# Attention scores that carry over in PSUM by differences of keys, with the maximum subtracted in the first two of eight key steps

## The reference

```
q = (x @ Wq.T).reshape(b, t, 8, 64)
kv_latent = x @ Wkv_down.T                       # 64 numbers for each token
k = (kv_latent @ Wk_up.T).reshape(b, t, 8, 64)
v = (kv_latent @ Wv_up.T).reshape(b, t, 8, 64)
scores = einsum('bqhd,bkhd->bhqk', q, k) * 64 ** -0.5
out = einsum('bhqk,bkhd->bqhd', softmax(scores, axis=-1), v)
return out.reshape(b, t, 512) @ Wo.T
```

## Time and profile before

| what | value |
|---|---|
| median of 3 runs | 1230.92 us (1229.14 to 1231.17) |
| profiled execution | 1230.1 us |
| its span (first to last instruction) | 1228.3 us |
| PE busy | 1016.4 us (83%), 5480 matmuls |
| DVE busy | 792.7 us (65%) |
| POOL busy | 676.9 us (55%) |
| ACT busy | 488.4 us (40%) |
| attention's blocks | from 237.7 us to about 1034 us of the span |

### The profile page before, as it was taken

The page is one execution under the profiler, slowest core; times in us unless marked ns, Lnnn a source line. Parts: engine busy times, 40 slices in busy tenths (PEclk is TensorE's granted clock), DMA queues, the critical chain, the costliest instruction groups (busy, mean ns, idle before and its releaser), DMA issues.

```text
span 1228.3 us, 17831 instructions
## 1 busy us (share of the span) xinstructions
PE 1016.4 (83%) x5480; PEld 586.1 (48%) x5481; DVE 792.7 (65%) x1211; ACT 488.4 (40%) x760; POOL 676.9 (55%) x385
## 2 busy tenths in 40 slices
PE   5839975499999989999998999998999999559800
PEld 4828842244444554444454444445455555538600
DVE  6565457657878746787873777877667744565431
ACT  1354431244444344444434444442445554344300
POOL 0025344277777627677644777773687785035371
PEclk9999956599999989999998999999999999669955
DMA  8055522000000100000010000001001000145453
GB/s 287 7 168 156 148 71 88 24 2 1 1 1 1 44 2 1 1 1 1 1 44 2 1 1 1 1 1 43 1 1 76 30 1 1 34 154 161 133 151 121
DMA packets 39484, 60.26 MB, mean 49 GB/s; under 512 B 5872, under 2 KB 33008, under 8 KB 38384
## 3 DMA queue, kind: packets, MB, share of 16 engines
q1 hardware_dynamic: 19424, 25.30, 5.8%
q0 software_dynamic: 6912, 18.88, 5.8%
q10 hardware_dynamic: 13072, 15.09, 3.5%
HBM read 30.81 MB, written 23.07 MB: 44 GB/s over the span
## 4 chain that ended last, share of the span: by engine, by line
PE 60%; DVE 11%; issue 9%; ACT 8%; POOL 7%; DMA 3%; ACTq 0%; DVEq 0%; POOLq 0%; SPq 0%
PE ps_o L928 14%; PE ps L913 9%; PE ps L560 6%; PE ps L720 5%; ACT arena_b L1120 5%; POOL arena_b L1322 5%; PE ps_x L700 4%; DVE maxes L726 3%; PE ps L916 3%; PE ps L1061 3%; PE ps L197 2%; PE ps_x L949 2%; ACT rows_store L476 2%; POOL arena_b L675 2%; PE ps L544 1%
## 5 line engine op out<-in xcount | busy, mean ns | idle before, releaser
L1322 POOL TENSOR_TENSOR arena_b<-arena_b 128x1024 f32<-128x1024 f32 x224 | 537.1, 2398 | 275.4 <-PE ps_o L928 168.7
L726 DVE TENSOR_REDUCE maxes<-ps 128x2 f32<-128x1024 f32 x256 | 311.7, 1218 | 184.0 <-PE ps L720 181.0
L1120 ACT ACTIVATE arena_b<-ps 128x1024 f32<-128x1024 f32 x256 | 255.8, 1024 | 190.7 <-PE ps L916 178.3
L928 PE MATMUL ps_o<-arena_b,latent_now 128*64 128x512 f32 x1024 | 261.6, 618 | 14.2 <-ACT arena_b L1120 5.3
L913 PE MATMUL ps<-q_split,keys_now 64*128 64x512 f32 x1536 | 223.5, 396 | 0.0
L509 POOL DMA_INDIRECT arena_b<-scaled_x,token_of x80 | 75.8, 947 | 178.5 <-issue 83.1
L913 PEld LDWEIGHTS ps<-q_split,keys_now 64*128 64x128 f32 x1536 | 147.1, 188 | 30.3 <-issue 2.4
L928 PEld LDWEIGHTS ps_o<-arena_b,latent_now 128*64 128x64 f32 x1024 | 53.1, 135 | 150.2 <-ACT arena_b L1120 132.9
L1239 DVE RECIPROCAL rows_store<-rows_store 128x256 f32<-128x256 f32 (+1 forms) x72 | 112.6, 1565 | 12.0 <-ACT rows_store L1131 12.0
L916 PE MATMUL ps<-q_shift 64*128 64x512 f32 x512 | 101.9, 393 | 0.0
L675 POOL DMA_INDIRECT arena_b<-sorted_y,slots x64 | 60.8, 950 | 67.2 <-DVE x_res L683 27.9
(11 more groups left out here) (175 smaller groups left out, 1127.1 us busy)
## 6 DMA issues: line engine op xcount, KB each, us to landing
sorted_y<-arena_b ACTq DMA_DIRECT2D x80, 128.0 KB
scaled_x<-rows_store SPq DMA_DIRECT2D x32, 256.0 KB, 2.1
x_res<-x_in SPq DMA_DIRECT2D x4, 1024.0 KB, 13.0
keys_now<-keys_next SPq DMA_DIRECT2D x4, 1024.0 KB, 4.6
out<-x_res SPq DMA_DIRECT2D x32, 128.0 KB
arena_a<-w_gu SPq DMA_DIRECT2D x1, 2048.0 KB, 16.0
arena_a<-w_gu ACTq DMA_DIRECT2D x1, 2048.0 KB, 7.7
arena_b<-scaled_x,token_of POOLq DMA_INDIRECT x80
```

Source lines behind the costliest of these rows:

```text
L726: nc.vector.tensor_reduce(maxes[:, 2 * m:2 * m + 2], ps[2][:, :, :], AX_X, ALU.max) \
L928: last = nc.tensor.matmul(ps_o[h, :], latent_now[:, kt, :], src, start=(kt == 0), stop=(kt == KT - 1))
L1120: nc.scalar.activation(dst, ps_s[n % 2][:, :, :], ACT.Exp, scale=SCALE).then_inc(sem("exp_done"), 1)
L1322: nc.gpsimd.tensor_tensor(t, t, probs[kt % PROBS].rearrange("p a n -> p (a n)"), ALU.add) \
```

## The change

The latents of key tile kt become differences: for kt = 0, 1 the key itself, from kt = 2 on the key minus the key 256 tokens (two tiles) before. As the two PSUM tiles are used in turn, tile kt is written on top of the scores of kt - 2 and not cleared; so the sum is again the score of kt, and the maximum subtracted in steps 0 and 1 stays in. The shift's pair (L916) is issued in steps kt = 0, 1 only, ahead of the other three. The maxima still need whole keys, which get tiles of their own. The differences are made by DVE from `row_pairs`, now in block 1, and take five instructions for half 0 and three for half 1.

```
+STRIDE = 2
+FIRST = STRIDE * P
+        q_shift = sb("q_shift", [P, SEQ + P], F32R)
+        keys_max_next = sb("keys_max_next", [P, SEQ], F32R)
+        keys_max_now = sb("keys_max_now", [P, SEQ], F32R)
+        key_diff = sb("key_diff", [P, HALF])
...
         def act_latents(act, nb, j, bank):
-            nc.scalar.activation(keys_next[:, 0, j * HALF:(j + 1) * HALF], bank, ACT.Copy).then_inc(sem("lat_hi"), 1)
+            nc.scalar.activation(keys_max_next[:, j * HALF:(j + 1) * HALF], bank, ACT.Copy).then_inc(sem("lat_hi"), 1)
-        def dve_keys_lo(dve, nb, j, bank):
-            nc.vector.tensor_tensor(keys_next[:, 1, cols], bank, keys_next[:, 0, cols].bitcast(F32), ALU.subtract) \
-                .then_inc(sem("lat_lo"), 1)
+        def dve_keys(dve, nb, j):
+            latent = row_pairs[:, :, :].rearrange("p j n -> p (j n)")
+            a = max(j * HALF, FIRST)
+            cols, back = slice(a, (j + 1) * HALF), slice(a - FIRST, (j + 1) * HALF - FIRST)
+            diff = key_diff[:, 0:(j + 1) * HALF - a]
+            dve.wait_ge(sem("lat_hi"), 2 * nb + j + 1)
+            if j == 0:
+                nc.vector.tensor_copy(keys_next[:, 0, 0:FIRST], keys_max_next[:, 0:FIRST].bitcast(F32)) \
+                    .then_inc(sem("key_hi"), 1)
+                nc.vector.tensor_tensor(keys_next[:, 1, 0:FIRST], latent[:, 0:FIRST],
+                                        keys_max_next[:, 0:FIRST].bitcast(F32), ALU.subtract) \
+                    .then_inc(sem("key_lo"), 1)
+            nc.vector.tensor_tensor(diff, latent[:, cols], latent[:, back], ALU.subtract).then_inc(sem("key_diff"), 1)
+            dve.wait_ge(sem("key_diff"), 2 * nb + j + 1)
+            nc.vector.tensor_copy(keys_next[:, 0, cols], diff).then_inc(sem("key_hi"), 1)
+            dve.wait_ge(sem("key_hi"), 3 * nb + j + 2)
+            nc.vector.tensor_tensor(keys_next[:, 1, cols], diff, keys_next[:, 0, cols].bitcast(F32), ALU.subtract) \
+                .then_inc(sem("key_lo"), 1)
         def pe_turn_latents(pe, nb, j, bank):
-            pe.wait_ge(sem("lat_f"), 2 * nb + j + 1)
-            pe.wait_ge(sem("lat_lo"), 2 * nb + j + 1)
+            pe.wait_ge(sem("lat_hi"), 2 * nb + j + 1)
...
-                    for key, query in ((k_hi, q_hi), (k_hi, q_lo), (k_lo, q_hi)):
+                    first = kt < STRIDE
+                    if first:
                         for a, h in enumerate(head_rows):
-                            nc.tensor.matmul(ps_s[n % 2][:, a, :], keys_now[h, key, k], query[h, p, q],
-                                             start=(key == k_hi and query is q_hi), stop=False)
-                    for a, h in enumerate(head_rows):
-                        last = nc.tensor.matmul(ps_s[n % 2][:, a, :], shift_ones[h, :], shift_row[h, q],
-                                                start=False, stop=True)
+                            nc.tensor.matmul(ps_s[n % 2][:, a, :], shift_ones[h, :], shift_row[h, q],
+                                             start=True, stop=False, skip_group_check=True)
+                    for key, query in ((k_hi, q_lo), (k_lo, q_hi), (k_hi, q_hi)):
+                        for a, h in enumerate(head_rows):
+                            last = nc.tensor.matmul(ps_s[n % 2][:, a, :], keys_now[h, key, k], query[h, p, q],
+                                                    start=False, stop=(kt >= KT - STRIDE and query is q_hi and key == k_hi),
+                                                    skip_group_check=True)
...
-                                pe_max(pe, (p + 1) % PAIRS, m, keys_next if p == PAIRS - 1 else keys_now,
+                                    if p == PAIRS - 1:
+                                        pe.wait_ge(sem("key_lo"), 3 * (b + 2))
+                                pe_max(pe, (p + 1) % PAIRS, m, keys_max_next if p == PAIRS - 1 else keys_max_now,
...
                         pieces(1)
-                        if not last_batch and p in (1, 2) and d == 0:
-                            dve_keys_lo(dve, b + 1, p - 1, ps_x[:, :])
+                        if not last_batch and p in (1, 2) and d == 1:
+                            dve_keys(dve, b + 1, p - 1)
...
-                for src, dst in ((keys_next, keys_now), (latent_next, latent_now)):
-                    sp.dma_start(dst[:, :, :].bitcast(F32), src[:, :, :].bitcast(F32)).then_inc(sem("batch_ready"), 16)
+                for src, dst in ((keys_next[:, :, :], keys_now[:, :, :]), (latent_next[:, :, :], latent_now[:, :, :]),
+                                 (keys_max_next[:, :], keys_max_now[:, :])):
+                    sp.dma_start(dst.bitcast(F32), src.bitcast(F32)).then_inc(sem("batch_ready"), 16)
+            sp.wait_ge(sem("key_lo"), 3)
```

More of the change, by code:

```diff
@@ L95, in build @@
         q_split = sb("q_split", [P, PAIRS, 2, SEQ], F32R)
-        q_shift = sb("q_shift", [P, 2, 2, SEQ], F32R)
+        q_shift = sb("q_shift", [P, SEQ + P], F32R)
+        keys_max_next = sb("keys_max_next", [P, SEQ], F32R)
+        keys_max_now = sb("keys_max_now", [P, SEQ], F32R)
+        key_diff = sb("key_diff", [P, HALF])
         w_qk = sb("w_qk", [P, DC, PAIRS, P])
@@ L132, in build @@
         k_hi, k_lo = 0, 1
-        shift_row, shift_ones = q_shift[:, 0, 0, :], q_shift[:, 0, 1, 0:P]
+        shift_row, shift_ones = q_shift[:, 0:SEQ], q_shift[:, SEQ:SEQ + P]
         gu_rows = arena_a[:, 0:4096]
@@ L720, in pe_max @@
                 last = nc.tensor.matmul(ps_m[a], q_hi[h, slot, qt * P:(qt + 1) * P],
-                                        keys[h, k_hi, half * HALF:(half + 1) * HALF], start=True, stop=True)
+                                        keys[h, half * HALF:(half + 1) * HALF], start=True, stop=True)
             last.then_inc(sem("max_scores"), 1)
@@ L800, in act_latents @@
             nc.scalar.activation(row_pairs[:, j, :], bank, ACT.Copy).then_inc(sem("lat_f"), 1)
-            nc.scalar.activation(keys_next[:, 0, j * HALF:(j + 1) * HALF], bank, ACT.Copy).then_inc(sem("lat_hi"), 1)
-        def dve_keys_lo(dve, nb, j, bank):
-            cols = slice(j * HALF, (j + 1) * HALF)
-            dve.wait_ge(sem("lat_hi"), 2 * nb + j + 1)
-            nc.vector.tensor_tensor(keys_next[:, 1, cols], bank, keys_next[:, 0, cols].bitcast(F32), ALU.subtract) \
-                .then_inc(sem("lat_lo"), 1)
+            nc.scalar.activation(keys_max_next[:, j * HALF:(j + 1) * HALF], bank, ACT.Copy).then_inc(sem("lat_hi"), 1)
[4 more added lines that the diff above has]
+            diff = key_diff[:, 0:(j + 1) * HALF - a]
+            dve.wait_ge(sem("lat_hi"), 2 * nb + j + 1)
+            if j == 0:
[10 more added lines that the diff above has]
+                .then_inc(sem("key_lo"), 1)
         def pe_turn_latents(pe, nb, j, bank):
-            pe.wait_ge(sem("lat_f"), 2 * nb + j + 1)
-            pe.wait_ge(sem("lat_lo"), 2 * nb + j + 1)
+            pe.wait_ge(sem("lat_hi"), 2 * nb + j + 1)
             for g in range(4):
@@ L882, in pe_attention @@
             for m in range(MAXES):
-                pe_max(pe, 0, m, keys_next, m, m == 0)
+                pe_max(pe, 0, m, keys_max_next, m, m == 0)
                 if m == MAXES // 2:
@@ L886, in pe_attention @@
             pe.wait_ge(sem("q_lo"), 4)
-            pe.wait_ge(sem("batch_ready"), 32)
+            pe.wait_ge(sem("batch_ready"), 48)
             pe.wait_ge(sem("q_fill"), 4)
@@ L1040, in batch @@
                         if p == 0 and d == 0:
-                            pe.wait_ge(sem("batch_ready"), 32 * b + 32)
+                            pe.wait_ge(sem("batch_ready"), 48 * b + 48)
                         if p or d:
@@ L1202, in dve_attention @@
             for j in range(2):
-                dve_keys_lo(dve, 0, j, banks[4 + j])
+                dve_keys(dve, 0, j)
                 gathered(QT + ROW_PAIRS + j)
@@ L1349, in sp_attention @@
             pairs(BATCH - 1, True)
-            sp.wait_ge(sem("batch_ready"), 32 * BATCH)
+            sp.wait_ge(sem("batch_ready"), 48 * BATCH)
             for c in range(2):
```

## The result

The changed kernel takes 1240.15 us (median of 6 runs, 1238.4 to 1245.29), the kernel before 1230.05 (6 runs, 1228.56 to 1233.3): ratio 1.0084, 95% interval 1.0063 to 1.0105. It is slower by 10 us, where 20 were forecast; the time lies in the range of 1226 to 1264. The profiled execution took 1240.86.

A forecast was written before the change was run, and what follows sets the result against it. Each block was bound by its chain of scores, exponential and values, or by POOL's adds, not by PE everywhere. 1230.1 - 11 - 1.2 - 0.8 + 27 + 6 = 1250.1, predicted 1250 us, range 1226 to 1264.

The forecast's parts named there:

- the stalls: Block 1, head pairs 1 and 2, three batches: PE 5.1 and 3.9 us late behind DVE's key work; 27 us lost.
- the clock: PE's granted clock falls after the stalls: 2 us for each of three long ones, nothing for the others; 6 us lost.
- Gain of the matmuls removed: Attention blocks with kt of 2 or more: 48 keep 0.23 us each from the dropped shift pairs; 11 us gained.
- the earlier transposes: Block 0, six times: transposes wait only for ACT's rounding and start 0.2 us sooner; 1.2 us gained.
- Rival B: PE sets every block, so all 44 us of removed matmuls are gained: 1186 us; chance 0.03.
- Where the second pair's 0.23 us go: Blocks losing two pairs: the second's 0.23 us becomes PE idle time before the values, about 0.2 more a block.
- Ahead of batch 0: Before batch 0 the transposes start sooner after ACT's rounding, with queries behind them on the path; 0.8 us gained.
- the middle of a tie: Half 1: the copy and POOL's add ready together; PE 2.7 us late if copy first, 5.1 if POOL; 3.9 taken.
- That the copy waits: Key work in block 1: DVE's copy of the difference waits for POOL's running add; if not, stalls cost 14 us.
- Rival A: Block 1's stalls don't come, as DVE works between POOL's adds or finishes before them: 1219 us; chance 0.13.

The follow-up runs named there:

- x1: The changed kernel with DVE's key work left out of the loop over batches: 1218.55 us, ratio 0.9882 to the kernel before.
- x3: The changed kernel with DVE's key work moved from block 1 to block 4 of the same head pairs: 1218.06 us, ratio 0.9880 to the kernel before.
- x9: The changed kernel with eight or four unused matmul passes added on PE in block 2, before the piece that waits: 1237.09 us, ratio 1.0057 to the kernel before.
- x2: The changed kernel with the shift's pair issued in every step again, adding: 1243.5 us, ratio 1.0088 to the kernel before.
- x5: The changed kernel with each of POOL's adds cut to 8 of 1024 columns: 1187.59 us.
- x6: The kernel before with each of POOL's adds cut to 8 of 1024 columns: 1204.87 us.

## Why the prediction was right, point by point

The mechanism came as forecast: DVE's key instructions wait for POOL's adds, and PE waits behind them. The loss was forecast at 20 us and measured at 10, so its size was off by half of the forecast; the stalls and the clock were priced too high, and a stall that the forecast didn't have made up 2 us of that, by luck.

- **Gain of the matmuls removed, 11 us, and of the earlier transposes, 1.2.** Measured 12.8 in all blocks but the stalls, and 11.5 to 14.2 in x1. Of the 12.8, 1.2 lie in block 0 of head pairs 1 and 2 (0.2 in each of six), which is the place of the transposes. A block keeps one pair, not two; a block held by POOL keeps nothing (block 6 of head pair 1, batch 1: 4.93 us before, 4.92 after). Rival B, PE as the only limit (1186), was wrong by 32 us even with the stalls taken out (x3).
- **Where the second pair's 0.23 us go.** The forecast had PE's idle time before the values grow by 0.2 us a block. That sign didn't come: PEld's waits there fell from 132.9 us to 122.5, PE's own rose from 5.3 to 10.3. What grew in the ordinary blocks is a wait that the forecast didn't have: the block's second piece of maxima now stands ready before DVE has reduced the first, and PEld's waits for DVE's maxima went from 31 times to 107. In those blocks it costs nothing that shows, as the values, which come later, start 0.23 us sooner all the same.

```profile
PEld ps_o L949 <- ACT arena_b L1143: 122.5, 201, 1.8
...
PE ps_o L949 <- ACT arena_b L1143: 10.3, 29, 0.9
```

- **Ahead of batch 0, 0.8 us.** 0.4 measured, which isn't told from nothing: in the traces of the changed kernel and of seven runs with the same code up to there, the first score matmul starts between 235.6 and 238.6 us.
- **The stalls, 27 us.** The step that was mis-sized: measured 22.1 with their aftermath and the clock in it, against 27 and the clock's 6. In half 0 I let the difference push POOL's first add to 501.1, 0.4 late, and gave the two adds 5.1 us: PE 5.1 us late. The add started on its time (2.21 us into the block), the two took 4.76, and PE was 4.2 late. In half 1 I took the middle of a tie; the copy won all three times by 0.1 us, and PE was 2.2 late, with 2.7 forecast for that case. 3 x (4.2 + 2.2) = 19 stands against the 27.
- **The clock, 6 us.** Right in kind: it fell to 1.2 GHz after each of the six stalls, the short ones too, which the forecast had at nothing. x9 puts the price at 3: 0.6 to 0.7 us behind a long stall, where I had 2, and 0.4 to 0.5 behind a short one. Why a long one costs so little wasn't followed up.
- **That the copy waits.** Shown: 2.38 us beside an add, 0.29 ahead of it (x2). The Trainium skill (GPSIMD Engine Reference, Key points) names contention between GpSimd and DVE's instructions in a two-port mode, and this trace agrees as far as the wait goes; which mode the copy ran in no run here shows.
- **Not in the sum:** the 2.0 us of the last batch's block 1. I had costed only instructions that the change adds; this one belongs to the old kernel, and merely met POOL's add at another moment.
- 1230.1 - 11 - 1.2 - 0.8 + 27 + 6 = 1250 against 1230.1 - 12.8 - 0.4 + 22.1 + 2.0 = 1241, with the clock's 3 us inside the 22.1. Rival A (DVE gets in between the adds) fell with the trace, but its time of 1219 is what the same change gives with the key work elsewhere (x3).

## What to carry to other kernels

Before moving work to an engine that is only 65% busy, look at which other engine runs at that moment: here some 1.75 us of DVE work, done six times, cost nothing in a block where POOL was idle at that moment (x3) and over 20 us in one where it wasn't, about three quarters of it by POOL's adds (x5). The price lies in who is queued behind, and dependent instructions pay once each, as the next add slips in between. An engine sped up upstream shifts who comes first, so walk every tie near the change again, those of old instructions too.

## What the runs showed of the hardware

- A DVE copy in SBUF from float32 to fp32r waits for POOL's add like an instruction with two SBUF inputs: 0.29 us for 256 columns alone, 2.38 us beside the add.
- Not every DVE instruction does. In the changed kernel the reductions of the maxima, from PSUM, took 1.23 us at the median both beside an add (136 times) and away from one, and the reciprocals, SBUF to SBUF, 1.74 both ways (51 times beside one).
- TensorE's granted clock fell to half after PE had stood for 2.3 us as well as for 4.3 (changed kernel, six times), and stayed full after 2.0 and 2.2 us (x2, six times).
- Small adds on POOL made the kernel before 26 us faster (x6), though ACT waited for adds for 11.1 us in its trace: what the adds do to DVE, and the waits behind that, are not in that line.
